# Two-layer graph attention: the order of a block of h and a chunk of products in PE's queue

## What is computed

```python
h = (x @ W).reshape(N, H, C)
al_s = jnp.einsum('nhc,hc->nh', h, a_src)
al_d = jnp.einsum('nhc,hc->nh', h, a_dst)
e = jax.nn.leaky_relu(al_s[src] + al_d[dst], NEG_SLOPE)
m = jax.ops.segment_max(e, dst, num_segments=N)
ex = jnp.exp(e - m[dst])
denom = jax.ops.segment_sum(ex, dst, num_segments=N)
alpha = ex / (denom[dst] + 1e-16)
msg = h[src] * alpha[:, :, None]
out = jax.ops.segment_sum(msg, dst, num_segments=N)
```

## Time and profile before

| what | us |
|---|---|
| median of 3 runs | 988.95 (988.51 to 989.52) |
| the profiled execution's own time | 991.75 |
| its span, first to last instruction | 989.80 |
| PE busy | 898.7 (91%) |
| DVE busy | 606.7 (61%) |
| ACT busy | 431.9 (44%) |
| POOL busy | 249.9 (25%) |

### The profile page before, as it was taken

One profiled execution on the slowest core, in us unless ns is written; L12 is line 12 of the kernel. 1 busy time (PEld: TensorE's weight loads), 2 busy tenths in 40 slices (PEclk: granted clock), 3 DMA queues, 4 the chain that ended last, 5 costly groups with the idle time before them and its releaser, 6 DMA issues.

```text
span 989.8 us, 15130 instructions
## 1 busy us (share of the span) xinstructions
PE 898.7 (91%) x5719; PEld 809.6 (82%) x5719; DVE 606.7 (61%) x1133; ACT 431.9 (44%) x704; POOL 249.9 (25%) x166
## 2 busy tenths in 40 slices
PE   4796676896999999999999999999999999789996
PEld 2354544686988899888988899899999999789996
DVE  9244464374788288964889449766212344488887
ACT  3644443316764366623865347754111111287400
POOL 1000003003931245302742229430000000054452
PEclk9997797998999999999999999999999999989998
DMA  8503995256145723657127522358214333210133
GB/s 295 123 1 65 153 148 139 77 166 198 51 148 176 199 80 108 201 121 214 62 61 218 143 99 61 112 141 226 62 47 86 65 58 54 54 44 1 43 100 93
DMA packets 64450, 111.18 MB, mean 112 GB/s; under 512 B 31772, under 2 KB 33464, under 8 KB 63004
## 3 DMA queue, kind: packets, MB, share of 16 engines
q1 hardware_dynamic: 62839, 107.09, 42.2%
q10 hardware_dynamic: 1540, 3.13, 1.2%
HBM read 85.25 MB, written 24.94 MB: 111 GB/s over the span
## 4 chain that ended last, share of the span: by engine, by line
PE 60%; DVE 17%; issue 7%; ACT 7%; POOL 4%; DMA 3%; SPq 1%; DVEq 1%; ACTq 0%; POOLq 0%
PE ps L1642 17%; PE ps L1644 17%; PE ps L1643 17%; DVE pbuf L586 4%; POOL pbuf L573 3%; PE ps L1673 3%; DVE vbuf L1375 2%; DVE PTlo L600 2%; DMA w1raw<-in_L_gnn_W 2%; PE ps L1762 2%; PE ps L1614 2%; DVE vbuf L1368 1%; PE ps L1604 1%; DVE h2f L1553 1%; DVE vbuf L1369 1%
## 5 line engine op out<-in xcount | busy, mean ns | idle before, releaser
L573 POOL TENSOR_TENSOR pbuf<-pbuf,grow 125x625 f32<-125x625 f32 x100 | 165.7, 1657 | 544.4 <-ACT pbuf L558 229.6
L1642 PE MATMUL ps<-hx,PThi 125*125 125x260 f32 (+5 forms) x800 | 229.8, 287 | 14.3 <-DVE PTlo L600 9.8
L1644 PE MATMUL ps<-hx,PTlo 125*125 125x260 f32 (+5 forms) x800 | 227.4, 284 | 0.0
L1643 PE MATMUL ps<-hlo,PThi 125*125 125x260 f32 (+4 forms) x800 | 227.1, 284 | 0.0
L1642 PEld LDWEIGHTS ps<-hx,PThi 125*125 125x125 f32 x800 | 151.1, 189 | 18.9 <-issue 12.1
L1643 PEld LDWEIGHTS ps<-hlo,PThi 125*125 125x125 f32 x800 | 151.6, 190 | 1.4
L1644 PEld LDWEIGHTS ps<-hx,PTlo 125*125 125x125 f32 x800 | 151.2, 189 | 0.0
L586 DVE SCALAR_TENSOR_TENSOR pbuf<-pbuf,counts 125x625 f32<-125x625 f32 x100 | 114.0, 1140 | 26.3 <-ACT pbuf L580 26.2
L595 ACT ACTIVATE PThi<-pbuf 125x625 fp32r<-125x625 f32 x80 | 58.0, 725 | 127.4 <-DVE pbuf L586 68.5
L1642 PE MATMUL ps<-W2p,hT 128*125 128x384 f32 x320 | 109.7, 343 | 3.2 <-DVE hT L1381 1.7
L600 DVE TENSOR_TENSOR PTlo<-pbuf,PThi 125x625 fp32r<-125x625 f32 x80 | 76.9, 961 | 51.3 <-ACT PThi L595 46.7
(11 more groups left out here) (184 smaller groups left out, 1682.0 us busy)
## 6 DMA issues: line engine op xcount, KB each, us to landing
xr<-xT_scratch SPq DMA_DIRECT2D x30, 750.0 KB, 4.8
nbm<-mask_scratch SPq DMA_DIRECT2D x40, 273.4 KB
hidden_scratch<-vbuf SPq DMA_DIRECT2D x40, 224.0 KB
hblk<-hidden_scratch SPq DMA_DIRECT2D x10, 896.0 KB
xT_scratch<-xa SPq DMA_DIRECT2D x20, 375.0 KB, 9.4
w1f<-in_L_gnn_W SPq DMA_DIRECT2D x12, 512.0 KB, 9.2
w1raw<-in_L_gnn_W SPq DMA_DIRECT2D x4, 1536.0 KB, 8.1
w2raw<-in_L_gnn_W SPq DMA_DIRECT2D x14, 384.0 KB, 5.5
```

The costliest lines, as they stand in the source:

```text
L573: pool.tensor_tensor(pslot(c), pslot(c), src[:, g * GN:(g + 1) * GN], ALU.add).then_inc(e_done, 1)
L1642: pe.matmul(dst, ahi, bhi, start=start, stop=False, skip_group_check=shared)
L1643: pe.matmul(dst[:, 0:n], ahi, blo, start=False, stop=False, skip_group_check=shared)
L1644: return pe.matmul(dst, alo, bhi, start=False, stop=stop, skip_group_check=shared)
```

## The change

In every second half except the last head's, PE's queue has block b of the next head's h ahead of chunk b where it had it behind. Nothing else is changed, on no other engine.

```diff
             for c in range(CHUNKS):
                 h, g, b = chunk_of(c)
-                chunk(c)
                 if g == 1 and h + 1 < H:
                     make(h + 1, b)
+                chunk(c)
                 if c == CHUNKS - 3:
                     transpose_h(0)
```

## The result

The changed kernel takes 1004.67 us (median of 4 runs, 1004.14 to 1005.36) against 988.73 us of the kernel before: 15.94 us longer, a ratio of 1.0165 with a 95% interval of 1.0147 to 1.0182. The forecast was 1005.0.

What follows compares the result with a forecast made beforehand. The prediction took operands made behind DVE's evictions to pace the first half, with PE stalling at handovers into second halves. Its terms, 12.5 - 0.6 - 6.5 + 10.7 = +16.1 us, gave a median of 1005.0 us, range 994 to 1012.

Steps and rivals of the forecast that it cites:

- Block 9 out of the handover: Handover from second to first half: left bare, while three second halves each grow by 4.18 us; +12.5 us, less 0.6.
- The first half's 0.6 saved: First half without block 9: its operands still pace it, so at best 0.6 us is saved, in one half.
- Block 0 into the handover: Handover from first to second half: block 0's 4.18 us cover all three eviction stalls; -6.5 us.
- The waits on h_lo: Second halves: each block waits for DVE's split of the block two before; +10.7 us together.
- block 2 of heads 1 and 2: Second half's start, DVE late with block 0's split: block 2 waits 1.9 us, twice, 3.8 in all.
- block 6: Behind DVE's longer step b = 7, which also makes the shift: a 1.0 us wait, three times, 3.0 in all.
- The ordinary steps: DVE's ordinary steps in second halves: PE late by 0.15 us at each of ten; 1.5 us.
- block 8, 2.4: Block 8 waits for block 6's split, held behind the next head's counts and the grow load; 2.4 us over three heads.
- The sum: Whole kernel: 12.5 - 0.6 - 6.5 + 10.7 = +16.1 us, so a median of 1005.0 us.
- (a): Rival: operands follow PE, so the bare handover costs only its evictions; -3.8 us, 985.1 us, chance 0.06.
- (b): Rival: block 9's cover is lost but no block waits for h_lo; +5.4 us, 994.4 us, chance 0.13.
- (c): Rival: slower still, by all steps as long as the last or new stalls lowering the clock; 1010 to 1014, chance 0.09.

Runs made afterwards that it cites:

- e2: The changed kernel with block 9 alone put back behind its chunk, into the handover from second to first half: 991.08 us.
- e7: e3 with, in step b = 9, also hx ahead of ACT's exp and hlo ahead of DVE's counts: 994.91 us.
- e1: The changed kernel with only block 0 of each new head ahead of its chunk, blocks 1 to 9 back behind theirs: 982.26 us.
- e3: The changed kernel with DVE's hlo between the two row maxima instead of behind both, in steps b = 3 to 7: 999.78 us.
- e4: The changed kernel with DVE's ELU in first halves cut to 8 of 512 columns: 997.57 us, one run.
- e6: e1 with the last head's blocks 1 to 7 one chunk later and its blocks 8 and 9 both behind chunk 59: 982.3 us.
- e5: The kernel before the change with DVE's ELU in first halves cut to 8 of 512 columns: 981.05 us, one run.

## Why the prediction was right

- **Block 9 out of the handover, +12.5 less 0.6.** Right: 12.7 (after against e2) and 13.0 (e7 against e1). The reading that decided it was 0.6 us of lead at chunk 29 in the earlier trace rows, and the forecast that its PTlo would be ready 35.77 us after chunk 19's end. DVE's timeline of after:

```profile
387.14 1.03 DVE L600 TENSOR_TENSOR PTlo<-pbuf,PThi 125x625 fp32r<-125x625 f32 x1 [0.79 <-ACT PThi L595]
...
391.91 0.15 DVE L1357 TENSOR_SCALAR deps<-ps 125x2 f32<-125x2 f32 x1
```

  It ends at 388.17, 35.76 us after chunk 19's end (352.41). The operands' chain did not move at all when a block in front of it vanished. *The first half's 0.6 saved* measured 0.5 in head 0 and nothing in the others.
- **Block 0 into the handover, -6.5.** Right: the stretches of e1 are 6.5 us shorter than before, its runs 5.6, and chunk 10 starts without a wait. The rule of the Trainium skill, Perfetto Trace Analysis, "Matmuls", that independent groups on other banks let evictions run beside them, agrees with the traces of e1 and after, where chunk 10 starts behind block 0 with no wait. It does not tell that after is slower (1004.7) where e1 is faster (982.3): after takes a block out of the other handover.
- **The waits on h_lo, +10.7.** The mechanism was right, the size somewhat high: 8.5 (after against e7) and 8.8 (e2 against e1) by the runs, 9.5 in the trace. By kind, from the starts of blocks in PE's timeline less the usual distance of 0.12: block 2 of heads 1 and 2 forecast at 3.8, measured 1.9 + 1.7; block 6 forecast at 3.0, measured 1.0 + 0.8 + 0.8. The split of block 0, forecast 17.35 us behind the start of the eviction, ends at 409.27 in after, 17.36 behind 391.91. The ordinary steps, forecast at 1.5, are 1.3: the waits before blocks 3 to 5, and before block 2 of head 0. The mis-sized term is *block 8, 2.4*: it measured 0.4 + 0.7 + 0. PE stood where the prediction had it: block 6 starts 0.65 us after the shift's end in each head. The other side of the sum came out otherwise. The split of block 6, which was taken to end 17.35 us after the shift as in head 1 of before, ends 16.6, 17.0 and 16.0 us after it in after (16.1, 17.3 and 17.2 in before), and the difference is in POOL's wait for grow, here of head 2 in before and then in after:

```profile
563.01 1.53 POOL L573 TENSOR_TENSOR pbuf<-pbuf,grow 125x625 f32<-125x625 f32 x1 [16.48 <-DMA grow<-shift_scratch]
```

```profile
574.25 1.53 POOL L573 TENSOR_TENSOR pbuf<-pbuf,grow 125x625 f32<-125x625 f32 x1 [15.26 <-DMA grow<-shift_scratch]
```

  Why the load came sooner there stays open. The waits before blocks add up to 8.6 of the 9.5 us; the rest was not told apart. *The expectation of e3* had an oversight of its own: it took the waits as independent, and with those of blocks 2 to 6 gone block 8's grew to 1.0 to 1.5 us.
- **The sum** is nearer than its terms. By the runs block 0 gained 0.9 us less than forecast, block 9 cost 0.8 to 1.1 more, the waits 1.9 to 2.2 less, and these cancel to 0.2 us (+16.1 forecast, +15.9 measured). Each miss is about as large as what a measurement can tell, but that they cancel is luck.
- **Rivals.** (a) wanted a first half of 36 us; after has 39.50 and 39.92. It needs operands that are ready, as in e4, and even there the time did not fall below before. (b) is e7, 994.9 where it had 994.4. (c), stalls that bring the lower clock, came up in e4 (below); in after the last stretch, 40.96 against 40.37, is the only one that grew without one of the three causes.
- **The profiled execution** of after is 13.6 us above that of before, the medians 15.9. The stretch from chunk 9 to chunk 79 has 15.8; chunk 9 itself ended 1.7 us earlier in after (272.40 against 274.07), ahead of all that the change touches.

What also stays open is how e6's 0.6 us would grow with a fourth buffer; it wasn't tried.

## What to carry to other kernels

A stall at a handover is covered by putting independent work there, but work that already stands at another handover may be hiding a slower producer: before moving it, look how long before its use the operand behind it is ready. That lead is the most that the old place gives back; the rest of the work's time is what the move costs. When one piece can be moved alone, move that one: here block 0 gains 5.6 us and the other nine lose 21.5. Waits along one queue don't simply add up: an earlier one can shield a later one, as in e3.

## What was not expected of the hardware

The clock fell after some short waits and not after others of about the same length. PE's timeline at chunk 70 and its window, before and then e1 (the last columns are the granted clock, DMA share and GB/s):

```profile
625.94 0.35 PE L1642 MATMUL ps<-hx,PThi 125*125 125x260 f32 x1 [1.85 <-DVE vbuf L1369]
...
625.94:631.48 5.54, 5.49 (x32) 5.23 (x33) 4.75 (x12) 2.13 (x4) 1.53 (x1) 0.69 0.00 0
```

```profile
617.60 0.36 PE L1642 MATMUL ps<-hx,PThi 125*125 125x260 f32 x1 [1.85 <-DVE vbuf L1369]
...
617.60:622.22 4.62, 4.31 (x30) 3.85 (x31) 4.55 (x12) 1.45 (x2) 1.53 (x1) 1.00 0.00 0
```

The wait is the same 1.85 us, and PE's starts show the three waits ahead of it as alike (0.80, 1.51 and 0.84 us from start to start in before, 0.81, 1.49 and 0.84 in e1), but before was granted 0.69 on average over the chunk, a mixture of both levels, and e1 stayed at 1.00; the chunk took 5.3 us in the one and 4.5 in the other. Over the nine traces it took 4.5 in e1 and e5 and 5.2 to 5.9 in the other seven; so the last column of the table compares kernels only with this in mind. In e4 one wait of 2.14 us before block 2 brought the lower level of 1.2 GHz, and the block took 5.5 us from its first matmul to its last instead of 4.1. A wait of 1.95 before block 2 of the head before, in the same trace, did not, nor did waits of 1.73 and 1.48 before the same blocks in after. The two of e4, the second with its window:

```profile
404.05 0.50 PE L1643 MATMUL ps<-W1hi,xr 128*125 128x512 f32 x1 [1.95 <-DVE hlo L1286]
...
523.12 0.79 PE L1643 MATMUL ps<-W1hi,xr 128*125 128x512 f32 x1 [2.14 <-DVE hlo L1286]
...
523.12:528.65 5.53, 5.53 (x18) 4.36 (x19) 5.39 (x8) 1.72 (x4) 1.87 (x1) 0.70 0.72 239
```

So a wait of this length can cost 0.8 to 1.5 us more than itself, and the traces of this case don't settle when it does.
